# A third of k's channels beside q in one bank, the rest of k in two 64-column tiles; k staged by 15 transfers instead of 9

## The reference, cut to what matters

```python
x = x + _L0_conv_ref(_gn(x), qkv_w, qkv_b, proj_w, proj_b, rel_table)   # shifted-window attention
x = x + _L1_conv_ref(_gn(x))                                           # ratio of box sums

# inside _L0_conv_ref: windows of 7 x 7 = 49 tokens, image rolled by 3, 12 heads of 8 channels
qkv = xw @ qkv_w.T + qkv_b
attn = einsum('bhqd,bhkd->bhqk', q * 8 ** -0.5, k) + bias + mask
out = einsum('bhqk,bhkd->bhqd', softmax(attn), v) @ proj_w.T + proj_b
```

## Time and profile before

| | us |
|---|---|
| median of three runs | 3295.98 |
| profiled execution, its own time | 3299.13 |
| its span | 3297.3 |
| TensorE (PE) busy | 3116.9 |
| VectorE (DVE) busy | 2809.8 |
| ScalarE (ACT) busy | 2384.0 |
| GpSimd (POOL) busy | 2259.2 |

### The profile page before, as it was taken

The page is one execution under the profiler, slowest core; times in us unless marked ns, Lnnn a source line. Parts: engine busy times, 40 slices in busy tenths (PEclk is TensorE's granted clock), DMA queues, the critical chain, the costliest instruction groups (busy, mean ns, idle before and its releaser), DMA issues.

```text
span 3297.3 us, 146814 instructions
## 1 busy us (share of the span) xinstructions
PE 3116.9 (95%) x60544; PEld 2641.3 (80%) x60544; DVE 2809.8 (85%) x4882; ACT 2384.0 (72%) x4705; POOL 2259.2 (69%) x2522
## 2 busy tenths in 40 slices
PE   4999999999999999999999999999999999999997
PEld 3778888888888888888888888888888888888885
DVE  4888888888888888888888888888888888888883
ACT  2577777777777777777777777777777777777774
POOL 4566767767767766767767667666677676677763
PEclk8999999999999999999999999999999999999995
DMA  3333333333333333333333333333333333332320
GB/s 86 79 87 85 94 85 86 94 84 87 93 86 87 92 86 85 92 88 86 92 86 85 91 89 86 87 91 83 88 94 83 86 94 83 86 96 73 75 64 24
DMA packets 385697, 280.20 MB, mean 85 GB/s; under 512 B 261931, under 2 KB 384908, under 8 KB 385036
## 3 DMA queue, kind: packets, MB, share of 16 engines
q1 hardware_dynamic: 384652, 270.69, 33.2%
q10 hardware_dynamic: 384, 0.11, 0.0%
HBM read 39.35 MB, written 38.54 MB: 24 GB/s over the span
## 4 chain that ended last, share of the span: by engine, by line
PE 59%; SPq 18%; ACT 8%; issue 7%; DMA 3%; DVE 3%; POOL 1%; ACTq 0%; DVEq 0%; POOLq 0%
PE pP L472 13%; PE pO L487 11%; SPq L335 8%; SPq L327 8%; PE pS L460 7%; PE pM L555 5%; DMA KE<-KS 3%; PE pM L572 3%; PE pM L561 3%; PE pM L442 3%; SPq L340 2%; ACT P L669 2%; PE pM L510 2%; PE pM L400 2%; PE pM L500 2%
## 5 line engine op out<-in xcount | busy, mean ns | idle before, releaser
L1061 POOL TENSOR_TENSOR T<-T,MX 128x588 f32<-128x588 f32 x1024 | 1214.2, 1186 | 532.4 <-DVE MX L832 531.5
L472 PE MATMUL pP<-K,T 113*128 113x113 f32 x6144 | 786.9, 264 | 41.7 <-ACT P L669 23.0
L825 DVE TENSOR_TENSOR T<-pS,table 128x588 f32<-128x588 f32 x1024 | 774.9, 757 | 42.3 <-PE pS L460 41.7
L832 DVE TENSOR_REDUCE MX<-T 128x12 f32<-128x588 f32 x1024 | 778.9, 761 | 27.0
L487 PE MATMUL pO<-V,P 128*49 128x18 f32 x24576 | 696.4, 197 | 50.4 <-ACT g L702 39.5
L472 PEld LDWEIGHTS pP<-K,T 113*128 113x128 f32 x6144 | 623.3, 141 | 128.3 <-issue 80.7
L669 ACT ACTIVATE P<-pP 128x588 f32<-128x588 f32 x1024 | 673.8, 658 | 68.3 <-PE pP L472 32.0
L487 PEld LDWEIGHTS pO<-V,P 128*49 128x49 f32 x24576 | 660.9, 126 | 57.6 <-ACT g L702 44.7
L1026 POOL TENSOR_TENSOR y<-Y 96x472 f32<-96x472 f32 x224 | 217.3, 970 | 482.0 <-ACT Y L746 482.0
L460 PE MATMUL pS<-KE,QS 128*64 128x196 bf16 (+1 forms) x8192 | 476.1, 233 | 21.3 <-DMA KE<-KS 13.7
L460 PEld LDWEIGHTS pS<-KE,QS 128*64 128x64 bf16 x8192 | 298.9, 109 | 136.5 <-issue 84.4
(11 more groups left out here) (94 smaller groups left out, 6034.5 us busy)
## 6 DMA issues: line engine op xcount, KB each, us to landing
KE<-KS SPq DMA_DIRECT2D x512, 147.0 KB
KS<-knh SPq DMA_DIRECT2D x768, 49.0 KB, 2.0
QS<-qnh SPq DMA_DIRECT2D x768, 49.0 KB
out<-tok_out SPq DMA_DIRECT2D x384, 84.0 KB
tok_in<-x SPq DMA_DIRECT2D x224, 84.0 KB
KS<-knl SPq DMA_DIRECT2D x384, 49.0 KB, 2.0
QS<-qnl SPq DMA_DIRECT2D x384, 49.0 KB
tok_in<-x SPq DMA_DIRECT2D x224, 63.0 KB
```

The lines of the kernel that those rows point to most:

```text
L472: mm = pe.transpose(pP[:, c, QN * at:QN * at + QN], T[j % 4][0:QN, 2 * h:2 * h + 2, :], pick)
L825: dve.tensor_tensor(T[j % 4][:, :, 0:L].rearrange("p (b h) k -> p b h k", b=2), pS[:, :, 0:HALF].rearrange("p b (h k) -> p b h k", k=L), t ...
L832: dve.tensor_reduce(MX[j % 4][:, :], T[j % 4][:, :, 0:L], AX.X, ALU.max).then_inc(maxed, 1)
L1061: pool.tensor_tensor(t, t, MX[j % 4][:, :].unsqueeze(2).broadcast_to([128, HEADS, L]), ALU.subtract).then_inc(shifted, 1)
```

## The change

q and k are now made in 64-column tiles of weights, which write to partitions 0 to 63 and 64 to 127 of a bank. `bankB` gets weight columns 0 to 127: q's 96 channels and, below them, k's first 32. `bankC` gets k's other 64 channels twice: tokens 0 to 195 of the unit in the upper tile, tokens 196 to 391 in the lower one. So q takes six matmuls of 392 columns in three pairs, k six of 196 columns in three pairs. ScalarE's copy and VectorE's subtraction cover 128 partitions; those of k are 196 columns long instead of 392. `kn` has 128 partitions and half the columns. In staging, k's first group comes from `qn`'s partitions 96 to 127 (three transfers), the other two groups from `kn`, each in two transfers by token halves (twelve transfers, with runs of 196 elements, 392 bytes). `stage` waits for `ql_made` ahead of k's transfers instead of between k's and q's.

```diff
+HALF_TOK = TOK // 2
...
-        qn = [[sb(f"qn{p}{i}", [C, 2 * TOK], BF16) for i in range(2)] for p in "hl"]
-        kn = [[sb(f"kn{p}{i}", [C, 2 * TOK], BF16) for i in range(2)] for p in "hl"]
+        qn = [[sb(f"qn{p}{i}", [128, 2 * TOK], BF16) for i in range(2)] for p in "hl"]
+        kn = [[sb(f"kn{p}{i}", [128, TOK], BF16) for i in range(2)] for p in "hl"]
...
                 sp.wait_ge(kl_made, 2 * S + 2)
+                sp.wait_ge(ql_made, 2 * S + 2)
...
                 for r, part in enumerate((0, 0, 1)):
-                    for gq in range(HG):
-                        sp.dma_start(KS[r:128:4, gq, :], kn[part][b][32 * gq:32 * gq + 32, :]
-                                     ).then_inc(k_stacked, 16)
-                sp.wait_ge(ql_made, 2 * S + 2)
+                    sp.dma_start(KS[r:128:4, 0, :], qn[part][b][C:128, :]).then_inc(k_stacked, 16)
+                    for gq in range(1, HG):
+                        of_unit = KS[r:128:4, gq, :].rearrange("p (u t n) -> p u t n", u=2, t=2)
+                        for t in range(2):
+                            at = 64 * t + 32 * (gq - 1)
+                            sp.dma_start(of_unit[:, :, t, :],
+                                         kn[part][b][at:at + 32, :].rearrange("p (u n) -> p u n", u=2)
+                                         ).then_inc(k_stacked, 16)
...
-                sp.wait_ge(k_stacked, 16 * 3 * HG * (S + 1))
+                sp.wait_ge(k_stacked, 16 * 3 * (2 * HG - 1) * (S + 1))
...
-            def project(dst, col, u, done):
-
-                xs = slice(TOK * u, TOK * u + TOK)
-                pe.matmul(dst[0:C, 0:TOK], WH[:, col:col + C], XH[:, xs], start=True, stop=False)
-                pe.matmul(dst[0:C, 0:TOK], WH[:, col:col + C], XL[:, xs], start=False, stop=False)
-                pe.matmul(dst[0:C, 0:TOK], WL[:, col:col + C], XH[:, xs], start=False, stop=True
-                          ).then_inc(done, 1)
+            def project(dst, tiles, done):
+
+                parts = ((WH, XH), (WH, XL), (WL, XH))
+                for part, (w, xs) in enumerate(parts):
+                    for half, (col, at, n) in enumerate(tiles):
+                        mm = pe.matmul(dst[64 * half:64 * half + 64, 0:n], w[:, col:col + 64], xs[:, at:at + n],
+                                       start=(part == 0), stop=(part == 2))
+                mm.then_inc(done, 1)
...
-                project(bankB, 0, u, q_made)
+                project(bankB, [(0, TOK * u, TOK), (64, TOK * u, TOK)], q_made)
...
-                project(bankC, C, u, k_made)
+                project(bankC, [(128, TOK * u, HALF_TOK), (128, TOK * u + HALF_TOK, HALF_TOK)], k_made)
...
-                act.activation(qn[0][b][:, s], bankB[0:C, 0:TOK], ACT.Copy).then_inc(qh_made, 1)
+                act.activation(qn[0][b][:, s], bankB[:, 0:TOK], ACT.Copy).then_inc(qh_made, 1)
...
-                act.activation(kn[0][b][:, s], bankC[0:C, 0:TOK], ACT.Copy).then_inc(kh_made, 1)
+                act.activation(kn[0][b][:, t], bankC[:, 0:HALF_TOK], ACT.Copy).then_inc(kh_made, 1)
...
-                dve.tensor_tensor(qn[1][b][:, s], bankB[0:C, 0:TOK], qn[0][b][:, s], ALU.subtract
+                dve.tensor_tensor(qn[1][b][:, s], bankB[:, 0:TOK], qn[0][b][:, s], ALU.subtract
...
-                dve.tensor_tensor(kn[1][b][:, s], bankC[0:C, 0:TOK], kn[0][b][:, s], ALU.subtract
+                dve.tensor_tensor(kn[1][b][:, s], bankC[:, 0:HALF_TOK], kn[0][b][:, s], ALU.subtract
```

More of the change, by code:

```diff
@@ L642, in high_qk @@
             def high_qk(U):
-                b, s = U // 2 % 2, slice(TOK * (U % 2), TOK * (U % 2) + TOK)
+                b, s, t = U // 2 % 2, slice(TOK * (U % 2), TOK * (U % 2) + TOK), slice(HALF_TOK * (U % 2), HALF_TOK * (U % 2) + HALF_TOK)
                 act.wait_ge(q_made, U + 1)
@@ L837, in low_q @@
                 dve.wait_ge(qh_made, U + 1)
-                dve.tensor_tensor(qn[1][b][:, s], bankB[0:C, 0:TOK], qn[0][b][:, s], ALU.subtract
+                dve.tensor_tensor(qn[1][b][:, s], bankB[:, 0:TOK], qn[0][b][:, s], ALU.subtract
                                   ).then_inc(ql_made, 1)
             def low_k(U):
-                b, s = U // 2 % 2, slice(TOK * (U % 2), TOK * (U % 2) + TOK)
+                b, s = U // 2 % 2, slice(HALF_TOK * (U % 2), HALF_TOK * (U % 2) + HALF_TOK)
                 dve.wait_ge(kh_made, U + 1)
-                dve.tensor_tensor(kn[1][b][:, s], bankC[0:C, 0:TOK], kn[0][b][:, s], ALU.subtract
+                dve.tensor_tensor(kn[1][b][:, s], bankC[:, 0:HALF_TOK], kn[0][b][:, s], ALU.subtract
                                   ).then_inc(kl_made, 1)
```

## The result

The changed kernel takes 3368.39 us, the median of four runs (3365.1 to 3377.91); the kernel before 3296.84, of four. The ratio is 1.0221, with a 95% interval of 1.0202 to 1.0241: slower. Forecast were 3320 us, range 3286 to 3385. The side was right and the time lies in the range, but the loss is 72 us and not 24: three times the forecast, and close to what the rival "SyncE becomes the bound" gave at 4.8 us per stage (3366).

A forecast was written before the change was run, and what follows sets the result against it. The prediction took a loop from TensorE's q through ScalarE and VectorE to the scores and back as the bound. 20.5 - 9.3 + 9 + 3.8 = +24 us on 3299.1 gave 3323, less 3.1 3320 us; range 3286 to 3385.

The forecast's parts named there:

- SyncE becomes the bound: Rival, chance 0.22: six more staging issues cost over 4.33 us per stage; at 4.8, +55 us and 3366 in total.
- The loop through q, not k: Ordinary unit's 12.17 us runs through q, its copy, low q and bias addition; k's shorter projection buys nothing there.
- The 0.05 us handoff: On TensorE, scores start 0.05 us after VectorE's bias addition ends, so they wait for it; this was to stay.
- The drain moved ahead of q: Switching from full-width matmuls to 64-column tiles now precedes q: 0.11 us per ordinary unit, +20.5 us in all.
- The norm units: Two units per image where TensorE waits for ScalarE: 0.15 us shorter each, -9.3 us in all.
- The packets' size: Staging's 392-byte runs within SBUF: 576 more packets per stage, counted at zero.
- no surcharge: On SyncE, a staging issue with 64 short runs was taken to cost no more than others.
- The start: First stage has no cover: six more issues at 0.64 us, +3.8 us.
- SyncE's queue: the step that failed: Six more staging issues, 4.3 us per stage, fill SyncE to 24.67 of 24.70 us; loss put at +9 us.
- the threshold of 4.33: SyncE becomes the bound when six more issues cost over 4.33 us per stage.
- the slack: Time between KE's last landing and the scores needing it: 8.8 us, forecast to shrink to 4.5.

The follow-up runs named there:

- after_act: The changed kernel with the stores' issues moved from SyncE's queue to ScalarE's: 3327.28 us, ratio 1.0073 to the kernel before.
- wide_act: The changed kernel with q and k's first third made by three full-width matmuls and the stores issued from ScalarE: 3306.61 us, ratio 1.0016.
- after_wide: The changed kernel with q and k's first third made by three full-width matmuls instead of six in 64-column tiles: 3377.99 us, ratio 1.0233.
- s12: The kernel before with one group of heads of k's staging cut by token halves, 12 transfers instead of 9: 3294.98 us, ratio 0.9982.
- s15u: The kernel before with k's staging in 15 transfers, two groups cut by units into runs of 784 bytes: 3346.01 us, ratio 1.0141.
- s15: The kernel before with only k's staging cut by token halves, 15 transfers instead of 9, runs of 392 bytes: 3383.92 us, ratio 1.0248.
- wide_store1: The changed kernel with full-width q and k's first third, and one store transfer per result group instead of two, all on SyncE: 3295.77 us, ratio 0.9991.

## Why the prediction was right and wrong

**The loop through q, not k: right.** The 0.05 us handoff stayed, the wait ahead of the scores became a row (0.26), and k's shortened projection bought nothing in ordinary units: with q at full width and k in tiles they take 12.17 us, not less than 12.16.

**The drain moved ahead of q: right.** 0.094 + 0.02 was forecast. Measured are 0.093 from the last transpose to q (0.190 instead of 0.097, the median of the ordinary units) and 0.03 in the projection, 0.13 per unit in all; in time 20.7 us (after_act against wide_act) where the queue has room. In the changed kernel itself it cost nothing that these runs can tell: after_wide takes it away and gains nothing.

**The norm units: right in direction, too small.** 0.15 each was forecast, 0.24 and 0.36 measured, 31 x 0.60 = 19 us and not 9. Medians over the 29 images, counted from the transposes ahead of q: q's copy starts 0.07 us later in both norm units (1.43 and 1.49 instead of 1.36 and 1.42) where I had 0.11, and the exponentials end 0.14 us earlier where I had 0.06. L521, now L530, starts 0.23 and 0.28 us earlier where I had 0.2, and nothing takes part of that back: TensorE goes on 0.23 and 0.28 us earlier. What makes the rest of the 0.36 was not looked for.

**The packets' size: right that the transfers don't suffer, wrong at zero.** The queue's share of the engines' time went from 33.2% to 33.6% with 86000 packets more, 672 per stage. I had 576, the runs alone; the other 96 are 16 for each of the six added issues, and s12 (336) and s15u (288) fit the same count. k's cut parts land in 1.9 us where the whole ones, of twice the bytes, took 2.0. Transfers of equal size land in 1.9 us with runs of 392 bytes (s15) and of 784 (s15u). The Trainium skill (DMA: Bandwidth & Descriptors, "Why small descriptors are slow (HBM only)") excepts transfers within SBUF, and the trace agrees. What I left out is the issue: 13 ns more for 64 runs, on SyncE's queue; my sum had "no surcharge".

**The start: too small.** 3.8 us forecast, 6.9 measured up to unit 16. I counted the first stage alone. The first images have no second block, their stages follow one another in 21 us, and SyncE falls behind at once: up to unit 16 TensorE waits for KE five times, 20.9 us, instead of once, 13.7. That the 21 us are the reason was not tried apart. The granted clock does not explain it: it was at its lower level for 27.3 us there before and for 3.4 after, which favours the changed kernel.

**SyncE's queue: the step that failed.** "I take **+9 us**" was the term; it measured 55. The balance was set up rightly, 20.37 us of work per stage against a period of 24.70, and rightly called full. Its price was off: 4.3 us for six issues, measured (100.7 - 81.6)/4 = 4.8. Two things make the 0.5. The added issues cost 0.73 us each with the gap, 4.4 per stage, in part the 13 ns of the split ones. And the 121 old ones of an image got dearer by 1.4 us, 0.35 per stage: those of q, KE and k by 2.6, loads and stores cheaper by 1.4, the gaps 0.2 more. The mean over a queue with pauses in it was no price for one without. Above the threshold of 4.33 that I gave, the loss is not the term itself but its excess times 128: 0.47 x 128 = 60 us, less the slack. s15 shows this cause alone (83 us with nothing but six more issues), s12 the threshold (three more cost nothing), after_act and wide_store1 the way back (issues taken off the queue return the loss). I named this as a rival and gave it 0.22; a balance that comes out at 99.9% should have had it as the forecast, since there is no room below it for an error of either sign to cancel.

**The total: luck in part.** 3368 lies in the range because the range reached over the rival, not because the forecast's sum held. And the rival's 3366 is nearer than its terms deserve: it adds 11 us of TensorE's side, which the full queue hides, and had the start too short.

## What to carry to other kernels

Count an in-order queue's whole work per period, gaps and slow issues included, before adding to it: three issues more were free here, six cost 2.5%. When the balance comes out near full, forecast the full queue, because an error of a few hundredths per issue multiplies with the number of periods. And place a change of TensorE's tile width behind whatever another engine waits for: q in tiles, with the change of width ahead of `q_made`, cost 0.13 us per unit; with q at full width and the change behind it nothing was lost (12.17 us against 12.16).

## What was not expected of the hardware

Issues on SyncE's queue got dearer as it filled: 0.692 instead of 0.673 us in the mean with the gap, in part because the added ones are of a dearer kind, with the median of those with 32 runs unchanged at 594 ns. One issue in ten takes over 0.8 us, 9.4% before and 10.5% after. In the changed kernel these slow ones recur in time: 348 of the 440 intervals between them are 5 to 8 us long. What makes them slow was not found. Sixteen issues per image on ScalarE cost 0.3%, more than half of it because four of them stand ahead of one copy that TensorE needs. And s12 is 0.18% faster than before with an interval that ends at 0.9991; its ordinary units are the same 12.16 us, its images 98.87 instead of 99.14, with fewer of the units that fall out of the pattern. Why stays open.
